# Gated attention: one copy of the keys without zero halves, scores on 64 partitions in two banks by turns, both heads' keys turned together

## The reference

```python
xn = (x - mu) / jnp.sqrt(var + LN_EPS) * gamma + beta
q = heads(xn @ Wq); k = heads(xn @ Wk); v = heads(xn @ Wv)
alpha = jax.nn.sigmoid(heads(xn @ Wa + ba))
knorm = jnp.linalg.norm(k, axis=-1, keepdims=True)
k = k / jnp.maximum(knorm, NORM_EPS)
def step(S, inp):
    q_t, k_t, v_t, a_t = inp
    S = a_t[..., None] * S + k_t[..., None] * v_t[..., None, :]
    o_t = jnp.einsum('bhji,bhj->bhi', S, q_t)
    return (S, o_t)
out = jnp.moveaxis(outs, 0, 1).reshape(Bx, Tx, D_INNER) @ Wo
return out + residual
```

## Time and profile before

| | |
|---|---|
| median of 3 runs | 1267.42 us (1258.23 to 1267.85) |
| the profiled execution, its own time | 1264.36 us |
| its span, first to last instruction | 1262.5 us |
| mean granted TensorE clock | 0.870 |
| PE busy | 1031.8 us (82% of the span) |
| DVE busy | 845.8 us (67%) |
| ACT busy | 382.9 us (30%) |
| POOL busy | 270.5 us (21%) |

### The profile page before, as it was taken

How to read it: one execution, slowest core, us unless ns; L and a number is a source line. 1 busy time by engine, 2 the same in 40 slices (tenths; PEclk the granted TensorE clock), 3 DMA queues, 4 the chain that set the end, 5 groups by cost and what they waited for, 6 DMA issues and landing times.

```text
span 1262.5 us, 16374 instructions
## 1 busy us (share of the span) xinstructions
PE 1031.8 (82%) x6027; PEld 638.2 (51%) x6027; DVE 845.8 (67%) x2101; ACT 382.9 (30%) x622; POOL 270.5 (21%) x231
## 2 busy tenths in 40 slices
PE   4898988989989788899978872899999566898465
PEld 2254555543434466683333331667768344676344
DVE  5676657756565586656777547548556896688896
ACT  1154444533333233223332225312211122231121
POOL 3600000003222211001222210310210243333232
PEclk8698888989989997759998986899999896787786
DMA  8623030020000000000000000000000000000000
GB/s 237 156 102 77 2 77 2 3 87 1 1 1 0 1 1 1 1 2 0 1 1 0 1 0 3 1 1 1 1 1 1 0 1 1 2 2 2 1 9 25
DMA packets 9948, 25.35 MB, mean 20 GB/s; under 512 B 979, under 2 KB 7315, under 8 KB 9171
## 3 DMA queue, kind: packets, MB, share of 16 engines
q1 hardware_dynamic: 9568, 23.44, 6.6%
q10 hardware_dynamic: 294, 0.79, 0.3%
HBM read 16.69 MB, written 7.34 MB: 19 GB/s over the span
## 4 chain that ended last, share of the span: by engine, by line
PE 53%; DVE 32%; issue 6%; ACT 3%; POOL 3%; DMA 2%; SPq 0%; DVEq 0%; ACTq 0%; POOLq 0%
PE ps L686 5%; DVE a_MN L359 4%; PE ps L673 4%; PE ps L678 3%; PE ps L252 3%; DVE XN L117 2%; DVE q_E L1252 2%; DMA a_QS<-a_MT 2%; POOL rs L96 2%; PE ps L194 2%; PE ps L1513 2%; PE ps L214 2%; PE ps L1467 2%; PE ps L1510 2%; PE ps L2043 2%
## 5 line engine op out<-in xcount | busy, mean ns | idle before, releaser
L359 DVE TENSOR_REDUCE a_MN<-ps 128x1 f32<-128x384 f32 (+3 forms) x176 | 107.6, 638 | 64.3 <-PE ps L197 62.0
L96 POOL TENSOR_TENSOR rs<-t,mhalf 128x4 f32<-128x4 f32 x37 | 37.4, 1010 | 409.4 <-DVE t L90 409.3
L930 POOL TENSOR_TENSOR f_Y<-f_Y,f_TT 128x512 f32<-128x512 f32 x56 | 70.9, 1266 | 178.5 <-DVE f_TT L820 178.5
L465 ACT ACTIVATE a_PT<-ps 128x1024 f32<-128x1024 f32 x64 | 65.1, 1025 | 72.4 <-PE ps L218 71.3
L143 DVE TENSOR_TENSOR X<-ps,X 128x512 f32<-128x512 f32 x32 | 22.0, 688 | 96.1 <-PE ps L1523 49.4
L895 ACT ACTIVATE f_HH<-ps,pack_zero 128x512 f32<-128x512 f32 x64 | 44.0, 687 | 132.8 <-PE ps L673 132.8
L194 PE MATMUL ps<-a_KS,a_QS 72*128 72x128 bf16 (+3 forms) x256 | 70.9, 339 | 13.6 <-DVE a_MN L359 10.4
L686 PE MATMUL ps<-f_HH,pack_zero 128*128 128x512 f32 x128 | 74.0, 661 | 5.7 <-DVE f_TT L820 5.7
L811 DVE TENSOR_TENSOR f_XS<-ps,XNT 128x512 f32<-128x512 f32 x64 | 43.9, 688 | 46.8 <-PE ps L666 46.8
L673 PE MATMUL ps<-f_XS,pack_zero 128*128 128x512 f32 x128 | 68.5, 618 | 1.3 <-DVE f_XS L811 1.3
L820 DVE SCALAR_TENSOR_TENSOR f_TT<-ps,pack_zero,f_X 128x512 f32<-128x512 f32 x64 | 47.9, 748 | 32.2 <-PE ps L686 32.2
(11 more groups left out here) (306 smaller groups left out, 2364.9 us busy)
## 6 DMA issues: line engine op xcount, KB each, us to landing
scratch<-a_parts SPq DMA_DIRECT2D x16, 384.0 KB, 4.3
a_QS<-scratch SPq DMA_DIRECT2D x3, 1152.0 KB
a_KS<-scratch SPq DMA_DIRECT2D x9, 384.0 KB
pack_one<-in_one SPq DMA_DIRECT2D x1, 2679.5 KB, 9.4
pack_zero<-in_zero SPq DMA_DIRECT2D x1, 2607.5 KB, 16.2
a_QS<-scratch SPq DMA_DIRECT2D x4, 288.0 KB
a_KS<-scratch SPq DMA_DIRECT2D x12, 96.0 KB
X<-in_x SPq DMA_DIRECT2D x4, 256.0 KB, 10.0
```

The lines of the kernel that those rows point to most:

```text
L96: pool.tensor_tensor(M.rs[:, 4 * b:4 * b + 4], M.t1[:, 4 * b:4 * b + 4], M.mhalf[:, 0:4], ALU.pow).then_inc(root.sem, root.tick(n, b))
L359: dve.tensor_reduce(M.a_MN[:, n % 2, ti, h0:h0 + k], bank(M, M.bank["a_max", n, jj], 128 * (ti + 1) * k).rearrange("p (a c) -> p a c", a=k ...
L465: act.activation(M.a_PT[:, c % 6, 0:1024], M.ps[:, a * 512:a * 512 + 1024], ACT.Exp).then_inc(made.sem, made.tick(n, hh))
L930: pool.tensor_tensor(M.f_Y[:, i, :], M.f_Y[:, i, :], M.f_TT[:, u % 3, :], ALU.add).then_inc(made.sem, made.tick(n, u))
```

## The change

- `h_KZ` loses its axis r. It holds each key once, [128, 4, 512], both heads of a group one above the other, without zeros. DVE writes it with 4 multiplications of 128 partitions for a batch where there were 8 of 64. The two memsets of POOL go.
- A score matmul contracts over the 64 partitions of its head. The two heads of a tile j are written in turns to two banks: for c = 0 to 3, first r = 0 and then r = 1. Both banks are taken before the first of the eight matmuls.
- The keys of a group are turned by one `transpose` of 128 x 128 (4 for a tile j) where there were 8 matmuls.
- The value products are issued in twos, after the pairs j = 2 and j = 3.
- DVE's `project(b)` waits also for the last turning of the batch before. The wait for the memsets at b = 0 goes; that for `h_R` stays.

```diff
     def scores(b):
...
-        for u in range(8):
-            j, r, scored, turned, value = u // 2, u % 2, S["h_scored"], S["h_kturn"], S["h_v"]
-            tk, bk = slice(128 * j, 128 * j + 128), spare()
-            M.bank["h_p", b, u] = bk
-            take(pe, M, bk)
+        for j in range(4):
+            tk, pair = slice(128 * j, 128 * j + 128), (spare(), spare())
+            for r in range(2):
+                M.bank["h_p", b, 2 * j + r] = pair[r]
+                take(pe, M, pair[r])
             for c in range(4):
-                m = pe.matmul(bank(M, bk, 128, 128 * c), M.h_KZ[:, r, c, tk], M.h_QZ[:, i, c, tk], start=True, stop=True)
-            m.then_inc(scored.sem, scored.tick(b, u))
-            M.freed[bk] = (S["h_pm"], (b, u))
-            if u > 3:
-                v, bk = u - 4, spare()
...
+                for r in range(2):
+                    row = slice(64 * r, 64 * r + 64)
+                    m = pe.matmul(bank(M, pair[r], 128, 128 * c), M.h_KZ[row, c, tk], M.h_QZ[row, i, c, tk], start=True, stop=True, skip_group_check=True)
+                    if c == 3:
+                        m.then_inc(scored.sem, scored.tick(b, 2 * j + r))
+            for r in range(2):
+                M.freed[pair[r]] = (S["h_pm"], (b, 2 * j + r))
+            if j > 1:
+                for v in (2 * j - 4, 2 * j - 3):
+                    bk = M.bank["h_v", b, v] = spare()
+                    take(pe, M, bk)
+                    pe.matmul(bank(M, bk), M.XNT[:, 512 * b + 128 * v:512 * b + 128 * v + 128], M.g_wv[:, :], start=True, stop=True).then_inc(value.sem, value.tick(b, v))
+                    M.freed[bk] = (S["h_vm"], (b, v))
+            if j < 3:
+                bk = M.bank["h_kt", b, j] = spare()
                 take(pe, M, bk)
                 for c in range(4):
-                    for q in range(2):
-                        m = pe.matmul(bank(M, bk, 64, 128 * c + 64 * q), M.h_KZ[:, q, c, tk], M.ident[:, 64 * q:64 * q + 64], start=True, stop=True)
+                    m = pe.transpose(bank(M, bk, 128, 128 * c), M.h_KZ[:, c, tk], M.ident[:, :])
...
     def project(b):
         kz, qz, clip = S["h_kz"], S["h_qz"], S["h_clip"]
         dve.wait_ge(S["h_ek"].sem, S["h_ek"].at(b))
-        if b == 0:
-            dve.wait_ge(S["h_zero"].sem, S["h_zero"].at(1))
-        else:
+        if b:
             dve.wait_ge(S["h_scored"].sem, S["h_scored"].at(b - 1, 7))
+            dve.wait_ge(S["h_kturn"].sem, S["h_kturn"].at(b - 1, 2))
         for c in range(4):
             bk = M.bank["h_k", b, c]
             dve.wait_ge(S["h_sq"].sem, S["h_sq"].at(b, c))
-            for r in range(2):
-                row = slice(64 * r, 64 * r + 64)
-                dve.tensor_tensor(M.h_KZ[row, r, c, :], bank(M, bk)[row, :], M.h_EK[row, c, :], ALU.mult).then_inc(kz.sem, kz.tick(b, c))
+            dve.tensor_tensor(M.h_KZ[:, c, :], bank(M, bk), M.h_EK[:, c, :], ALU.mult).then_inc(kz.sem, kz.tick(b, c))
...
 def tiles_gpsimd(pool, S, M):
     zero, made = S["h_zero"], S["h_pow"]
-    pool.memset(M.h_KZ[64:128, 0, :, :], 0.0).then_inc(zero.sem, zero.tick(0))
-    pool.memset(M.h_KZ[0:64, 1, :, :], 0.0).then_inc(zero.sem, zero.tick(1))
-    pool.wait_ge(zero.sem, zero.n)
-    pool.memset(M.h_R[:, :, :, :], 0.0).then_inc(zero.sem, zero.tick(2))
+    pool.memset(M.h_R[:, :, :, :], 0.0).then_inc(zero.sem, zero.tick(0))
```

More of the change, by code:

```diff
@@ L1455, in scores @@
     def scores(b):
-        i = b % 2
+        i, scored, turned, value = b % 2, S["h_scored"], S["h_kturn"], S["h_v"]
         pe.wait_ge(S["h_kz"].sem, S["h_kz"].at(b, 3))
@@ L1459, in scores @@
         if b == 0:
-            pe.wait_ge(S["h_zero"].sem, S["h_zero"].at(2))
-        for u in range(8):
-            j, r, scored, turned, value = u // 2, u % 2, S["h_scored"], S["h_kturn"], S["h_v"]
-            tk, bk = slice(128 * j, 128 * j + 128), spare()
-            M.bank["h_p", b, u] = bk
-            take(pe, M, bk)
-            for c in range(4):
-                m = pe.matmul(bank(M, bk, 128, 128 * c), M.h_KZ[:, r, c, tk], M.h_QZ[:, i, c, tk], start=True, stop=True)
-            m.then_inc(scored.sem, scored.tick(b, u))
-            M.freed[bk] = (S["h_pm"], (b, u))
-            if u > 3:
-                v, bk = u - 4, spare()
[L1472 to L1478, removed]
+            pe.wait_ge(S["h_zero"].sem, S["h_zero"].at(0))
@@ L1607, in states @@
         if b == 0:
-            dve.wait_ge(S["h_zero"].sem, S["h_zero"].at(2))
+            dve.wait_ge(S["h_zero"].sem, S["h_zero"].at(0))
         for j in range(3):
@@ L2385 @@
 GATED = {"g_C": ([128, B, 4, 512], F32), "g_NB": ([128, 4], F32), "g_top": ([128, 2], F32), "g_flag": ([1, 1], I32)}
-TILES = {"h_EK": ([128, 4, 512], F32), "h_KZ": ([128, 2, 4, 512], F32), "h_QZ": ([128, 2, 4, 512], F32), "h_PP": ([128, 8, 4, 128], F32),
+TILES = {"h_EK": ([128, 4, 512], F32), "h_KZ": ([128, 4, 512], F32), "h_QZ": ([128, 2, 4, 512], F32), "h_PP": ([128, 8, 4, 128], F32),
          "h_KT": ([128, 4, 512], F32), "h_V": ([128, 2, 4, 512], F32), "h_R": ([128, 3, 4, 128], F32), "h_A": ([128, 4, 64], F32),
```

## The result

The changed kernel takes **1273.99 us** (median of 20 runs, 1267.44 to 1278.47), the kernel before in the same comparison 1267.08 us (20 runs, 1258.23 to 1272.5). The ratio is 1.0057, its 95% interval 1.004 to 1.0074: about 7 us slower, outside the range that was given. Ratios leave out executions that are more than 1.5% above the fastest of their kernel (one each in experiments 4 and 11, two in experiment 8, one of the kernel before); medians are of all.

The account below looks back on a forecast made before the run. PE held 53% of the chain, but DVE was taken to set the pace in batches 1 and 2. Gains 3.5 + 1.1 + 1.1 + 2.4 = 8.1 us, less 3.5 for the clock, took 1264.4 to 1260 us; range 1250 to 1270.

Parts of the forecast that it names:

- The memsets: at b = 0 DVE had waited for ACT's square ... not for POOL: Start of batch 0: removing POOL's memsets was costed at nothing, because DVE had waited for ACT's square until 795.19.
- the forecast of 4.6 us faster: Whole kernel: net gain, 8.1 us from the four batches less 3.5 us for the clock.
- The clock term: PE's stalls among the scores: half-clock loss of 1.0 in batches 1 and 2, 0.75 in 0 and 3; bounds 0 and 6.8.
- From the start of n2 to the next scores unchanged: Stretch behind the key products, n2 to the next batch's scores: it would take as long as before.
- The slower rival: Batches 1 and 2: clock still down at the key products, 11 us a batch; 1271 or 1282 us, chance 0.12.
- Gains by batch: Scores to n2, or to output in batch 3: 3.5, 1.1, 1.1 and 2.4 us for batches 0 to 3.
- that DVE, not PE, sets the pace of the scores in batches 1 to 3: Scores of batches 1 and 2: DVE keeps its times, so most of PE's 7 us a batch becomes waiting.
- the two stalls: Batches 1 and 2, before the pairs j = 2: PE idle behind h_PP and h_KT, some 3 us each.
- the keys at 2.48: DVE's key multiplications: four of 128 partitions take 2.48 us a batch where eight halves took 5.73.
- The third stall, before j = 3: Last score pair in batches 1 and 2: PE idle behind h_PP before j = 3; no separate size given.
- Sizes: PE's scores and turning: pair 0.93 us, four transposes 0.49; V1 to n2 8.8, to output in batch 3 5.3.

Follow-up runs that it names:

- experiment 4: Changed kernel with POOL's addition held back and the 64-row scores one head after the other, one bank at a time: ratio 1.007 to the kernel before, 1278.17 us.
- experiment 11: Changed kernel, POOL's addition held, DVE's factors one batch ahead, fillers before two value products, n2 64 columns wide: ratio 0.9833 to the kernel before, 1245.22 us.
- experiment 8: Changed kernel, POOL's addition held, DVE's factors one batch ahead, first query product in the middle of n2: ratio 0.9934 to the kernel before, 1259.28 us.
- experiment 1: Changed kernel with POOL's addition X + XN held back until DVE's factors of batch 0 are done: ratio 0.9992 to the kernel before, 1266.29 us.
- Experiment 3: Changed kernel with POOL's addition held and PE's stalls filled with 512-column matmuls whose result nobody reads: ratio 0.9949 to the kernel before, 1260.41 us.
- experiment 10: Changed kernel, POOL's addition held, DVE's factors one batch ahead, n2 64 columns wide: ratio 0.9858 to the kernel before, 1247.52 us.
- experiment 2: Kernel before with its memsets kept but put behind POOL's addition X + XN: ratio 1.0025 to the kernel before, 1270.97 us.
- experiment 5: Changed kernel with POOL's addition held and DVE's factors computed one batch ahead: ratio 0.9923 to the kernel before, 1256.36 us.
- experiment 7: Changed kernel with POOL's addition held and the keys turned by eight matmuls again, from the single keys: ratio 1.0012 to the kernel before, 1268.78 us.
- experiment 6: Kernel before with DVE's factors computed one batch ahead, POOL's addition not held: ratio 0.9985 to the kernel before, 1266.72 us.
- experiment 9: Changed kernel, POOL's addition held, DVE's factors one batch ahead, one filler before each of the first two value products of batches 1 to 3: ratio 0.9911, 1255.13 us.
- experiment 12: Kernel before with n2 64 columns wide and nothing else: ratio 0.9992 to the kernel before, 1263.97 us.

## Why the prediction was wrong

- **The step that failed** is "The memsets: at b = 0 DVE had waited for ACT's square ... not for POOL", costed at nothing. It asked who waited for the memsets, and not what they held back. Their removal moved POOL's addition from 9.8 to 6.1 us behind g_flag, onto DVE's factors; 3.8 us in the trace before n2 begins (17.5 from g_flag against 13.7), and about 8 us by the runs of experiment 1 against after. No rival had it. With it the forecast of 4.6 us faster becomes 1 us faster by the traces' 3.8, and 3 us slower by the runs' 8. The rest of the miss is mostly the clock.
- **The clock term was mis-sized.** It was 3.5 us with 6.8 as its bound. In the profile it is about 10: some 5 behind the stalls (V1 starts 1.0 and 1.5 us later after the first score than before in batches 1 and 2, and 2.6 later than forecast in batch 0), 3.6 behind n2, and 1.5 in the first query products. The bound counted one half-clock stretch a batch, behind the stalls, and "From the start of n2 to the next scores unchanged" failed. There was a second stretch behind the n2 of batches 1, 2 and 3, where before it was behind those of 2 and 3, and it was longer behind that of batch 2 (6.7 us for the query products against 5.2). Experiment 3 gives back the first kind, experiment 10 the second. Part of the 3.6 can be chance: in the profile of experiment 2 the kernel before takes 25.7 us from n2 to the scores in batch 0, not 22.4. But all 20 executions of after had a mean granted clock of 0.844 to 0.860, where the kernel before, beside the experiments, had 0.858 to 0.875 in all but one. The slower rival had the right engine and the wrong place: the clock was back before the key products.
- **Gains by batch.** Batch 3, without factors and without keys behind, gave 1.9 where 2.4 was said. Batches 1 and 2 lost 0.5 and 1.1 where a gain of 1.1 each had been expected before the clock. Batch 0 gave 0.2 for 3.5: its third pair waits for ACT's copy as reckoned, but then takes 2.0 us for 0.93 and the two values behind it 3.3 for 1.7.
- **Right:** that DVE, not PE, sets the pace of the scores in batches 1 to 3, so that most of what PE gives up (26.7 us, 28.7 were said) turns into waits (16.9 us more idle time; experiments 5 and 7); the places and sizes of the two stalls (about 3 us each); the keys at 2.48. The third stall, before j = 3, came in batch 3 alone (1.71 us): in batches 1 and 2 work at half clock fills its place.
- **Sizes:** a pair is 1.10 us, 0.93 was taken from 32-partition rows; transposes 0.58 for 0.49. From the start of V1 to n2 it takes 9.3 to 9.4 us where 8.8 was said, and in batch 3 5.9 to the output for 5.3. That is 2.2 us in all: 0.7 from the four pairs, the rest from value products at 1.82 a pair for 1.72 and from 0.2 to 0.4 us between V1's start and the pair.
- **The sum.** From 4.6 faster to 8.5 slower in the stage are 13.1 us: 3.8 for the addition, 6.6 for the clock beyond the 3.5 taken, 2.2 for the sizes, and about 0.4 because the prediction took its ends of before from the chain, where they stand 0.1 to 0.2 us later than in the timeline.

The parts are not strictly additive: the intervals of the experiments are 6 to 12 us wide, and which spell of low clock falls on the path varies between executions.

## What to carry to other kernels

When an instruction is deleted, look at what stood behind it on its queue and what that will now run beside, even if nobody waited for the deleted one. A saving on an engine that then waits must be charged with the clock behind the wait and behind thin work; a filler or wider operands that cost no time can be worth more than the saving. A change that measures as nothing or as a loss may still pay once what holds it back is removed; to say what it is worth then, give the kernel before the same measures, all at once.

## What was not expected of the hardware

- A DVE instruction of 16 columns takes 4.43, 4.46 or 4.25 us instead of 0.18 when it meets a POOL addition of 4.5 us; all three times it ends with the addition.
- Norm matmuls of 2 and of 64 moving columns take the same 3.8 us for 32 records, but the clock behind them differs. Over the profiles of before, after and experiments 1 to 7 and 9, the query products behind the narrow n2 of batches 1 to 3 took 5.2 us or more 28 times of 30; behind the wide ones of experiments 10 to 12 the clock stayed at 1.00 all nine times.
- Single 64-row score matmuls with full-size products between them stayed at 0.50 for 15 us with PE busy throughout.
